# Maxima of attention scores begun on half of the keys, with turns of rows in halves and the output projection in quarters

## The reference

```
x: (4, 512, 256)   ctx: (4, 1024, 256)   mask: (4, 1024)   16 heads of 16
q = layernorm(x) @ w_q.T ; k = ctx @ w_k.T ; v = ctx @ w_v.T
q, k = rope(q), rope(k)
scores = q k^T / 4, -10000 where mask == 0
x = x + (softmax(scores) v) @ w_o.T
# then: layernorm, causal attention over the first axis, router,
# top 2 of 8 experts with GELU, added to x
```

## Time and profile before

| what | value |
| --- | --- |
| median of 3 runs | 857.69 us (856.13 to 857.75) |
| the profiled execution: time, span | 855.98 us, 854.2 us |
| PE busy | 695.6 us (81%) |
| DVE busy | 566.6 us (66%) |
| ACT busy | 493.7 us (58%) |
| POOL busy | 363.1 us (43%) |
| HBM | 82.11 MB read, 70.70 MB written |

### The profile page before, as it was taken

One profiled execution on the slowest core, in us unless ns is written; L12 is line 12 of the kernel. 1 busy time (PEld: TensorE's weight loads), 2 busy tenths in 40 slices (PEclk: granted clock), 3 DMA queues, 4 the chain that ended last, 5 costly groups with the idle time before them and its releaser, 6 DMA issues. The chain is left out here.

```text
span 854.2 us, 12963 instructions
## 1 busy us (share of the span) xinstructions
PE 695.6 (81%) x4120; PEld 412.9 (48%) x4120; DVE 566.6 (66%) x972; ACT 493.7 (58%) x954; POOL 363.1 (43%) x272
## 2 busy tenths in 40 slices
PE   4347899998999998999888988457876329999996
PEld 3233334443444434443333332356766318888885
DVE  5947767778777787778687842348687614555553
ACT  2011457778677775777666776265553226666663
POOL 4973606176034580043898920000143522445434
PEclk9675779999999999999899998568879558999999
DMA  9674453967458651238788820298312835523321
GB/s 266 210 206 139 167 171 96 292 192 231 141 167 237 211 160 72 77 97 228 233 281 269 281 116 1 68 362 332 44 66 63 277 93 134 108 33 38 37 31 19
DMA packets 60261, 133.31 MB, mean 156 GB/s; under 512 B 8996, under 2 KB 25940, under 8 KB 58740
## 3 DMA queue, kind: packets, MB, share of 16 engines
q1 hardware_dynamic: 33396, 73.51, 26.1%
q0 software_dynamic: 17360, 37.92, 17.1%
q10 hardware_dynamic: 9440, 21.06, 8.7%
HBM read 82.11 MB, written 70.70 MB: 179 GB/s over the span
## 5 line engine op out<-in xcount | busy, mean ns | idle before, releaser
L713 DVE TENSOR_REDUCE mx<-wide 128x2 f32<-128x1024 f32 x256 | 305.4, 1223 | 97.4 <-PE wide L836 96.9
L581 ACT ACTIVATE probs<-narrow 128x512 f32<-128x512 f32 x512 | 279.2, 598 | 102.4 <-PE narrow L863 100.6
L863 PE MATMUL narrow<-qst,kst 51*128 51x512 f32 x512 | 191.3, 468 | 12.5 <-ACT probs L581 6.4
L836 PE MATMUL wide<-kst,qst 49*128 49x512 f32 x512 | 159.7, 475 | 22.9 <-DVE mx L713 10.1
L863 PEld LDWEIGHTS narrow<-qst,kst 51*128 51x128 f32 x512 | 81.5, 191 | 170.0 <-ACT probs L581 114.6
L878 PE MATMUL values<-probs,vaug 128*17 128x512 f32 x1024 | 141.3, 625 | 0.7 <-ACT probs L581 0.7
L1557 POOL DMA_INDIRECT out<-res,token x39 | 60.9, 1560 | 99.4 <-DMA out<-res,token 62.0
L836 PEld LDWEIGHTS wide<-kst,qst 49*128 49x128 f32 x512 | 67.7, 197 | 45.6 <-DVE mx L713 29.0
L431 POOL TENSOR_TENSOR turn_b<-turn_a,tab 128x1024 f32<-128x1024 f32 x10 | 24.1, 2410 | 118.3 <-ACT turn_a L575 117.8
L1130 POOL DMA_DIRECT2D out<-h x4 | 5.3, 1337 | 129.5 <-DVE h L1313 129.5
L1582 ACT ACTIVATE h_hi<-narrow 128x512 fp32r<-128x512 f32 x39 | 23.3, 597 | 46.0 <-PE narrow L1659 46.0
(11 more groups left out here) (253 smaller groups left out, 1305.2 us busy)
## 6 DMA issues: line engine op xcount, KB each, us to landing
list_rows<-in_w ACTq DMA_DIRECT2D x56, 342.0 KB, 4.6
kst<-k_pieces SPq DMA_DIRECT2D x14, 784.0 KB
k_pieces<-turn_a SPq DMA_DIRECT2D x16, 512.0 KB, 4.8
w_hi<-w_hi SPq DMA_DIRECT2D x16, 512.0 KB
w_lo<-w_lo SPq DMA_DIRECT2D x16, 512.0 KB
qst<-q_pieces SPq DMA_DIRECT2D x14, 384.0 KB
turn_a<-in_w POOLq DMA_DIRECT2D x10, 512.0 KB, 5.7
w_hi<-turn_b POOLq DMA_DIRECT2D x10, 512.0 KB, 3.0
```

Source lines behind the costliest of these rows:

```text
L581: nc.scalar.activation(probs[:, n % NP, :], narrow[ring_no["score", n] % 3][:, :], ACT.Exp, scale=DK ** -0.5).then_inc(exp_done, 1)
L713: last = nc.vector.tensor_reduce(mx[quad % 2][:, qt, :, hp, kh], slot[:, :, :], axis=AX.X, op=ALU.max)
L836: last = nc.tensor.matmul(slot[:, i, :], qst[u % 3][r:r + R_MAX, h, P * qt:P * qt + P], kst[u % 3][r:r + R_MAX, h, 512 * kh:512 * kh + 512 ...
L863: nc.tensor.matmul(narrow[ring_no["score", n] % 3][:, :], kst[u % 3][r:r + R_ALL, h, P * kt:P * kt + P], qst[u % 3][r:r + R_ALL, h, :], st ...
```

## The change

- The transfers of the identity and of the mask are issued earlier, and the mask's job on VectorE stands behind the transposes of the input.
- The maxima of a quad take all blocks of the half of the keys with number 1 first and then those of number 0. In the opening the first eight wait only for the queries and half 1 (`quad_in`, four transfers), the other eight for half 0 (`half_in`, two transfers).
- The four k jobs of batch 1 are placed between the maxima of quad 0, and the split of its second context block goes before its first rotation. SyncE's list is rearranged to fit: the store of the part turned last comes before the mask row and the second pair of queries, and the context of batch 1 before the keys.
- Four maxima of quad 1 are moved into the opening. Maxima of quads 2 to 15 end one group earlier.
- Jobs xT and oT are split in two halves (of 128 of the 256 columns), each with its own PSUM slot; oP in four quarters of one query tile.
- Eight products of the identity with itself, of 128 columns, into `values` come before the first score.

The diff, cut to its core (job lists, transfers and the split jobs; waits that only take the new indices are left out):

```diff
-LEAD = 3
+AHEAD = 4
+
+
+def lead(quad):
+    return 3 if quad == 1 else 4
+
+
 GROUP_COST = 2.3
-JOB_COST = {"q": 1.4, "k": 1.4, "v": 1.4, "oP": 1.4, "xT": 1.0, "oT": 1.0, "out": 0.5}
+JOB_COST = {"q": 1.4, "k": 1.4, "v": 1.4, "oP": 1.3, "xT": 0.5, "oT": 0.5, "out": 0.5}
...
-        return [("max", quad, hp, qt, kh) for hp in range(2) for qt in range(QT) for kh in range(2)] + [("nm", quad), ("mxt", quad)]
-
-    before = [("rate", 0), ("xn", 0), ("w", "q"), ("c", 0, 1), ("w", "k"), ("mask", 0), ("xT", 0), ("k", 0, 1, 0), ("k", 0, 1, 1), ("rope", 0, 1), ("c", 0, 0),
+        return [("max", quad, hp, qt, kh) for kh in (1, 0) for hp in range(2) for qt in range(QT)] + [("nm", quad), ("mxt", quad)]
+
+    first = maxes(0)
+    before = [("rate", 0), ("xn", 0), ("w", "q"), ("c", 0, 1), ("w", "k"), ("xT", 0, 0), ("xT", 0, 1), ("mask", 0), ("k", 0, 1, 0), ("k", 0, 1, 1), ("rope", 0, 1), ("c", 0, 0),
               ("q", 0, 0), ("q", 0, 1), ("rope", 0, 2), ("k", 0, 0, 0), ("k", 0, 0, 1), ("rope", 0, 0), ("w", "v"), ("w", "o")]
     before += [("v", 0, g, n) for g in range(2) for n in range(2)]
-    before += [("rate", 1), ("c", 1, 0), ("k", 1, 0, 0), ("k", 1, 0, 1), ("rope", 1, 0), ("c", 1, 1)] + maxes(0)[:16]
-    before += [("k", 1, 1, 0), *maxes(0)[16:], ("k", 1, 1, 1), ("rope", 1, 1)]
+    before += [("rate", 1), ("c", 1, 0), ("c", 1, 1), *first[:3], ("k", 1, 0, 0), *first[3:5], ("k", 1, 0, 1), ("rope", 1, 0), *first[5:11], ("k", 1, 1, 0),
+               *first[11:13], ("k", 1, 1, 1), ("rope", 1, 1), *first[13:], *maxes(1)[:AHEAD]]
...
-        timed += [(g + 5.8, ("xn", t)), (g + 7, ("xT", t)), (g + 8.5, ("q", t, 0)), (g + 10, ("q", t, 1)), (g + 10, ("rope", t, 2))]
+        timed += [(g + 5.8, ("xn", t)), (g + 6.9, ("xT", t, 0)), (g + 7.1, ("xT", t, 1)), (g + 8.5, ("q", t, 0)), (g + 10, ("q", t, 1)), (g + 10, ("rope", t, 2))]
...
-        timed += [(g + 2.2, ("oT", b)), (g + 3.5, ("oP", b, 0)), (g + 5.5, ("oP", b, 1))]
+        timed += [(g + 2.7, ("oT", b, 0)), (g + 3.3, ("oT", b, 1))] + [(g + x, ("oP", b, n)) for n, x in enumerate((4.1, 4.7, 5.3, 6.1))]
...
-        first, last = when(max(8 * (quad - 1) - LEAD, 0)), when(8 * quad - LEAD)
-        todo = maxes(quad)
+        first, last = when(8 * (quad - 1) - lead(quad - 1) if quad > 1 else 0), when(8 * quad - lead(quad))
+        todo = maxes(quad)[AHEAD if quad == 1 else 0:]
         timed += [(place(first + (last - first) * n / (len(todo) - 1)), j) for n, j in enumerate(todo[:-1])] + [(place(last) + 0.6, todo[-1])]
...
+FIRST_WARM = 8
...
-        def landed(u, heads):
-            return quad_in if u == 0 and heads.start == 0 else stack_in[u % 3]
+        def landed(u, heads, parts=(0, 1)):
+            if u > 0 or heads.start != 0:
+                return stack_in[u % 3]
+            return half_in if parts == (0,) else quad_in
...
         load_x(0)
+        sp.dma_start(mask_i[:, :], io["mask"]).then_inc(mask_in, 16)
         load_context(0, 1)
         load_table(0)
         sp.dma_start(turn_b[1][:, :, :], io["ctxT"][:, 0:512].rearrange("(k p) t -> p k t", p=P)).then_inc(first_in, 16)
         load_keep(0, 1)
-        sp.dma_start(mask_i[:, :], io["mask"]).then_inc(mask_in, 16)
         load_table(1)
...
-        load_keep(1, 0)
         load_queries(0, slice(0, 2))
         load_keys(0, slice(0, 2), (1,))
+        store_turned(0, 0)
+        load_keep(1, 0)
+        load_context(1, 1)
+        load_keys(0, slice(0, 2), (0,))
         load_queries(0, slice(2, PAIRS))
-        store_turned(0, 0)
-        load_keys(0, slice(0, 2), (0,))
         load_keys(0, slice(2, PAIRS))
-        load_context(1, 1)
...
+        act.dma_start(ident[:, :], io["ident"]).then_inc(ident_in, 16)
         load_weight("q")
         load_weight("k")
-        act.dma_start(ident[:, :], io["ident"]).then_inc(ident_in, 16)
...
-                dst, src = xT_hi[:, :, :], slot[:, :, :]
+                dst, src = xT_hi[:, j[2], :], slot[:, 0, :]
...
-                last = nc.vector.tensor_tensor(xT_lo[:, :, :], slot[:, :, :], xT_hi[:, :, :].bitcast(F32), ALU.subtract)
+                last = nc.vector.tensor_tensor(xT_lo[:, j[2], :], slot[:, 0, :], xT_hi[:, j[2], :].bitcast(F32), ALU.subtract)
...
-                xb = xt[:, QT * b + 2 * n:QT * b + 2 * n + 2, :]
-                last = nc.vector.tensor_tensor(xb, slot[:, 0, :].rearrange("p (t d) -> p t d", d=D), xb, ALU.add)
+                xb = xt[:, QT * b + n, :]
+                last = nc.vector.tensor_tensor(xb, slot[:, 0, 0:D], xb, ALU.add)
...
-                b, n = j[1:]
-                for i in halves:
-                    t = 2 * n + i
-                    last = product(slot[:, 0, D * i:D * i + D], transposed(slice(P * t, P * t + P)), weight("o"))
+                t = j[2]
+                last = product(slot[:, 0, 0:D], transposed(slice(P * t, P * t + P)), weight("o"))
...
-                for k in range(KC):
-                    for t in range(QT):
-                        last = nc.tensor.transpose(slot[:, k, P * t:P * t + P], xn[:, t, P * k:P * k + P], ident[:, :])
+                k = j[2]
+                for t in range(QT):
+                    last = nc.tensor.transpose(slot[:, 0, P * t:P * t + P], xn[:, t, P * k:P * k + P], ident[:, :])
...
-                if (quad, hp, qt, kh) == (0, 0, 0, 0):
-                    pe.wait_ge(quad_in, 96)
-                if (hp, qt, kh) == (0, 0, 0) and (quad % 2 == 0 and quad > 0 or quad == 1):
+                if (quad, hp, qt) == (0, 0, 0):
+                    pe.wait_ge(*((quad_in, 64) if kh == 1 else (half_in, 32)))
+                if (hp, qt, kh) == (0, 0, 1) and (quad % 2 == 0 and quad > 0 or quad == 1):
...
-            if g == 0:
-                pe.wait_ge(values_prepared, 3)
...
+        pe.wait_ge(values_prepared, 3)
+        for i in range(FIRST_WARM):
+            nc.tensor.matmul(values[:, 0:P], ident[:, :], ident[:, :], start=True, stop=True)
```

More of the change, by code:

```diff
@@ L96, in attention_order @@
     steps = [steps_of(g) for g in range(GROUPS)]
-    after = [("moments", 0), ("out", QUADS - 1), ("oT", B - 1), ("oP", B - 1, 0), ("oP", B - 1, 1)]
+    after = [("moments", 0), ("out", QUADS - 1), ("oT", B - 1, 0), ("oT", B - 1, 1)] + [("oP", B - 1, n) for n in range(QT)]
     order = before + [j for now in steps for what, j in now if what in ("job", "finish")] + after
@@ L101, in attention_order @@
     for b in range(1, B):
-        assert index[("xT", b)] < index[("out", 4 * (b - 1))]
-        assert b < 2 or index[("oT", b - 2)] < index[("xn", b)] and index[("oP", b - 2, 1)] < index[("xT", b)]
-        assert index[("q", b, 1)] < index.get(("oT", b - 1), len(order))
+        assert index[("xT", b, 1)] < index[("out", 4 * (b - 1))]
+        assert b < 2 or index[("oT", b - 2, 1)] < index[("xn", b)] and index[("oP", b - 2, QT - 1)] < index[("xT", b, 0)]
+        assert index[("q", b, 1)] < index.get(("oT", b - 1, 0), len(order))
         assert all(index[("v", b - 1, g, 1)] < index[("c", b, g)] for g in range(2))
     return order, index, before, steps, after
+FIRST_WARM = 8
 FILL = 684
@@ L345, in load_keys @@
             for i in range(2):
-                sp.dma_start(kst[u % 3][HALF * i:HALF * i + R_MAX, heads, tokens].bitcast(F32), k[i][:, heads, tokens]).then_inc(landed(u, heads), 16)
+                sp.dma_start(kst[u % 3][HALF * i:HALF * i + R_MAX, heads, tokens].bitcast(F32), k[i][:, heads, tokens]).then_inc(landed(u, heads, parts), 16)
         def load_table(half):
@@ L661, in _ @@
                 if b == 1:
-                    dve.wait_ge(*by_pe(("xT", 0)))
+                    dve.wait_ge(*by_pe(("xT", 0, 1)))
                 elif b > 1:
-                    dve.wait_ge(*by_pe(("oT", b - 2)))
+                    dve.wait_ge(*by_pe(("oT", b - 2, 1)))
                 for t in range(QT):
@@ L715, in _ @@
                 quad = j[1]
-                dve.wait_ge(*by_dve(("max", quad, 1, QT - 1, 1)))
+                dve.wait_ge(*by_dve(("max", quad, 1, QT - 1, 0)))
                 step(nc.vector.tensor_reduce(nm[:, :, :, :], mx[quad % 2][:, :, :, :, :], axis=AX.X, op=ALU.max, negate=True))
@@ L727, in _ @@
                 if b > 0 and first == 0:
-                    dve.wait_ge(*by_pe(("oT", b - 1)))
+                    dve.wait_ge(*by_pe(("oT", b - 1, 1)))
                 if first == 0 and b + 1 < B:
-                    dve.wait_ge(*by_pe(("xT", b + 1)))
+                    dve.wait_ge(*by_pe(("xT", b + 1, 1)))
                 if j[1] > 0:
@@ L768, in project_inputs @@
             if kind == "q" and j[2] == 0:
-                pe.wait_ge(*by_dve(("xT", j[1])))
+                pe.wait_ge(*by_dve(("xT", j[1], 1)))
                 pe.wait_ge(*by_splitter(("w", "q")))
@@ L776, in project_inputs @@
             elif kind == "oP":
-                pe.wait_ge(*by_dve(("oT", j[1])))
+                pe.wait_ge(*by_dve(("oT", j[1], 1)))
                 pe.wait_ge(*by_splitter(("w", "o")))
@@ L848, in job @@
                 pe.wait_ge(*by_dve(("out", 4 * j[1] + 3)))
```

(6 more changed lines are left out.)

4 lines of the change are left out of this document (2 added, 2 removed).

## The result

The changed kernel takes **874.67 us** (median of 4 runs, 871.43 to 896.09) beside 857.72 of the kernel before on the same chip: **1.019** of it, 95% interval 1.014 to 1.024. I had said 832. The profiled execution took 871.43 us, span 869.6, against 855.98 and 854.2 before.

A forecast was written before the change was run, and what follows sets the result against it. TensorE bounds the long middle; in the opening VectorE's maxima delay the scores. Terms -6.1 -6.1 -2.0 -5.0 -4.1 -1.2 sum to -24.5 us, from 855.98 to 831.5, given as 832 for the median; range 821 to 846.

The forecast's parts named there:

- First 21 us: Start of the kernel: identity and mask issued earlier bring the end of VectorE's statistics 1.0 us sooner (0.45 to 1.6).
- First maxima: Maxima of quad 0: first reduced at 48.8 instead of 61.90, four k jobs costing 4 us, end at 71.0 instead of 80.09.
- fourth rival: Opening: second half of the keys lands as late as before, at 61, maxima stop after eight; 834 to 836; chance 0.05.
- To the first score: From last maximum to first score: warming products put 3 us on the path; first score at 79.5, before 85.65, -6.1 us.
- Groups 0 to 4: First attention groups: 12 maxima instead of 16, 17.5 us instead of 23.6, -6.1 us (ends -4.5 and -9.5).
- Groups 5 and 6: The two groups after the first five run at the full clock: -2.0 us (0 to -3).
- Steady state, halves and quarters: Later groups: turns in halves and projection in quarters shorten slot holds and stalls, -5.0 us (0 to -9).
- second rival: Steady state: waits only change their names, a half turn waiting for a reduction, the quarter for its slot; 841; chance 0.12.
- Lead and maximum rows: Later quads: maxima ending one group sooner cover most of a 3.2 us wait for maximum rows, -4.1 us (-1 to -5).
- End: End of the kernel: halves let VectorE begin earlier and the last add shrinks, -1.2 us (-0.3 to -1.6).
- fifth rival: Groups with halves and quarters: TensorE falls to half its clock, 5.0 us instead of 2.59 each; 861 to 904; chance 0.03.

The follow-up runs named there:

- x_lead4_halves: Kernel before plus the changed opening, lead 4 for every quad from 2 on, turns in halves, projection in two blocks: 866.31 us against 858.0, ratio 1.008.
- a_proj_two: Changed kernel with the output projection in two blocks again, the same kernel as `x_lead4_halves` on another chip: 868.04 us, ratio 1.013 to the kernel before.

## Why the prediction was wrong

The opening gave less than I said, and the steady state lost where I had booked a gain: at weighing 10 the lead was 4.45 us and not 14.2, and from weighing 10 to 127 the kernel took 20.3 us more where halves, quarters and lead were to take 9.1 off. By the prediction's steps, in the profiled executions:

- **First 21 us.** Transposes at 9.67 (said 10.3), mask wait gone: right. The end of the statistics moved by 0.0 us, not 1.0: too large even at my lower end of 0.45. The row of 2.82 us beside GpSimd shows it: that step ends at 26.98, 0.54 behind the end of a GpSimd step of 2.67 us (23.77 to 26.44), and GpSimd had begun no sooner. The Trainium skill, SBUF — State Buffer, "Who interferes with whom" says that a VectorE instruction with two SBUF inputs contends with a GpSimd one that reads SBUF, for a shared port pair that is an exclusive lock; I weighed this rule and took the larger value. The trace agrees with it here, and in group 11 in the step of 1.18 us.
- **First maxima.** First reduction at 49.82 (48.8), the four k jobs at 5.82 us (4), the last maximum at 74.42 (71.0). The keys turned last landed by 61.64, not by 56 to 57.5: my step that less traffic before their store would bring them 3 us sooner failed, and the fourth rival was right on that point. The eight maxima ahead covered it but for 0.70 us.
- **To the first score.** Warming on the path 2.6 us (3). First score 2.1 us sooner, not 6.1: 1.0 from the first reduction, 0.6 from longer reductions (18.8 for 18.2), 1.8 from the k jobs, 0.6 behind the last.
- **Groups 0 to 4.** From the first score to weighing 4 -5.9 (said -6.1, ends -4.5 and -9.5); -4.8 of it between weighings 0 and 4. Right.
- **Groups 5 and 6.** +3.5 to weighing 7 and +3.6 to weighing 10 instead of -2.0. I had booked 1 us of gain for each turn of the input in halves. The turn of the input waited 2.70 us in group 6 for its normalized rows; the kernels at lead 3 with whole turns took 24.6 to 26.0 us from 4 to 10.
- **Steady state, halves and quarters.** 33 to 34 took 3.70 us (I said near 5), but 34 to 38 took 7.2 more. The gain was given back in the next four groups and more: worse than the second rival, which had the stalls only change their names. I had priced the pieces by the slots that they free and not by the maxima that the lead brings into the same groups.
- **Lead and maximum rows.** The wait is gone, -5.3 at 86 to 88 (said -4.1). Nowhere did I ask where `nm` and `mxt` would fall: three times into the rotation, 2.3 us each, and once beside GpSimd's splitting of weights, at the head of the loss of 13.0 us from 98 to 102; nor that the lead's maxima would lie beside the quarters. The step that failed is this pair of terms, -5.0 for halves and quarters and -4.1 for the lead: each was priced as if the other were not there and with the clock kept. Their sum came out at +20.3 instead of -9.1, while with the changed opening each alone costs nothing (0.991, 0.995 and 0.996 beside 0.996).
- **End.** From weighing 127 to the first norm 14.14 us (before 15.35): -1.2, as said.
- **The clock.** The fifth rival, a clock that falls in the groups with halves and quarters, was the outcome in kind, at 875 instead of 904. I gave it 0.03 on the ground that the clock had held from 147.6 to 404 through all the old waits. That reading was wrong. The waits in that stretch were of at most 1.1 us, and the longest of the earlier trace rows, 3.2 us, lies just behind its end. Timeline and stretch of the kernel before:

```profile
407.63 0.80 PE L863 MATMUL narrow<-qst,kst 51*128 51x512 f32 x2 [3.25 <-DMA qst<-mxp]
```

```profile
408.00:415.00 7.00, 7.00 (x33) 2.45 (x31) 3.88 (x5) 4.45 (x8) 6.41 (x7) 0.64 0.57 187
```

  The clock did fall there, to a mean of 0.64. A rival that needed "24 us" was also judged against an inflated gain: against the real one of the opening, 4 to 5 us by the medians, two such groups of 2.4 us suffice.

## What to carry to other kernels

When a due time moves, list what every job after it now lies beside, on every engine, before pricing what it frees: here one group of lead was free by itself behind the changed opening, as was each finer piece, and together they cost 2%. Price a wait of a busy TensorE twice, with the clock kept and with the clock lost, and put a chance on the second. Give a longer lead only to the load that was late: lead 4 for quad 11 alone stands at 0.987, lead 4 for all of them at 0.996.

## What the runs showed of the hardware

- VectorE's steps of 16 elements, 0.17 us alone, took 0.84 and 1.18 us beside GpSimd's rotation and 2.23 us (L733, at 452.84) beside one GpSimd step of 2.38.
- A wait of 2.3 us of TensorE left the clock at 1.00 in one execution of a kernel (`x_lead4_halves`) and at a mean of 0.72 over the 12.10 us around it in another of the same kernel (`a_proj_two`). A wait of 2.18 us, up to 456.26, went with 13.7 us at 0.50 (changed kernel, 455.3 to 469.0).
- On one core the same kernel varied by 2% from run to run (843.6 to 860.4 us at lead 3 with halves and quarters), with a mean granted clock of 0.907 in the fastest and 0.884 in the slowest.
- Eight FP32 products of 128 columns took 3.51 us at a mean clock of 0.55 (sixteen records).
